# A transformer layer with routed experts: scatters issued one in a round, two PSUM banks for the shared experts' sums, and VectorE making one of the two copies that swap a query's halves

## What is computed

```python
x = x + attention(layernorm(x), freqs_cis, Wq, Wkv_a, kv_gamma, kv_beta, Wkv_b, Wout)
x = x + moe(layernorm(x), gate_w, w_gate, w_up, w_down, sw_gate, sw_up, sw_down)

# inside the attention, for each query
def _rope(x, theta):
    x1, x2 = (x[..., 0::2], x[..., 1::2])
    c, s = (jnp.cos(theta), jnp.sin(theta))
    return jnp.stack([x1 * c - x2 * s, x1 * s + x2 * c], axis=-1).reshape(x.shape)

# inside the mixture: 8 experts, each token goes to its 2 best, and all go through a shared expert
scores = jax.nn.softmax(x @ gate_w, axis=-1)
topk_w, topk_idx = jax.lax.top_k(scores, K)
routed = jnp.einsum('teh,ehd,te->td', silu(gate) * up, w_down, comb)
shared = jax.nn.silu(x @ sw_gate) * (x @ sw_up) @ sw_down
```

## Time and profile before

| | |
|---|---|
| runs | 649.59, 646.07, 648.93 us; median 648.93 |
| the profiled execution | 649.52 us, its span 647.7 us |
| TensorE's mean granted clock | 0.979 of full |
| TensorE busy, matmuls / weight loads | 611.8 us / 594.9 us |
| VectorE, ScalarE, GpSimd busy | 470.3, 475.8, 407.9 us |
| head, until about | 50 us |
| middle loop, until about | 489 us |
| shared expert for batches 0 to 3, until about | 529 us |
| expert tiles, until about | 614 us |

### The profile page before, as it was taken

How to read it: one execution, slowest core, us unless ns; L and a number is a source line. 1 busy time by engine, 2 the same in 40 slices (tenths; PEclk the granted TensorE clock), 3 DMA queues, 4 the chain that set the end, 5 groups by cost and what they waited for, 6 DMA issues and landing times. The chain is left out here.

```text
span 647.7 us, 15727 instructions
## 1 busy us (share of the span) xinstructions
PE 611.8 (94%) x4916; PEld 594.9 (92%) x4916; DVE 470.3 (73%) x1406; ACT 475.8 (73%) x1331; POOL 407.9 (63%) x455
## 2 busy tenths in 40 slices
PE   8989999999899989989999999998987889999995
PEld 7879999999899989989999999998977879999995
DVE  6666786887666877778688887777676676666577
ACT  4669899899688979879888987987864435555531
POOL 2467888786877799689779968967602204444400
PEclk9998999999899999999999999999889999999999
DMA  9891000000100000010000001010302146444283
GB/s 251 250 330 25 2 2 2 2 34 1 35 2 33 26 10 34 2 35 3 34 34 2 34 1 35 1 67 33 123 34 74 70 128 190 130 126 123 84 301 105
DMA packets 34025, 45.41 MB, mean 70 GB/s; under 512 B 4057, under 2 KB 29113, under 8 KB 33945
## 3 DMA queue, kind: packets, MB, share of 16 engines
q1 hardware_dynamic: 29160, 34.56, 17.0%
q0 software_dynamic: 3408, 9.34, 4.4%
q10 hardware_dynamic: 1376, 0.50, 0.3%
HBM read 27.57 MB, written 16.82 MB: 69 GB/s over the span
## 5 line engine op out<-in xcount | busy, mean ns | idle before, releaser
L1239 ACT ACTIVATE probs<-ps_s,nmax 128x256 f32<-128x256 f32 x256 | 119.1, 476 | 10.5 <-DVE nmax L1429 10.2
L1774 POOL TENSOR_TENSOR qswap<-qswap,qsin 128x512 f32<-128x512 f32 x64 | 83.0, 1297 | 50.0 <-ACT qswap L1216 49.8
L224 PE MATMUL ps_q<-xa,wq_hi 128*128 128x256 f32 x512 | 103.0, 299 | 3.1 <-DVE qf L1424 3.1
L1429 DVE TENSOR_REDUCE nmax<-ps_s 128x2 f32<-128x512 f32 x128 | 86.8, 678 | 13.8 <-PE ps_s L224 12.8
L1216 ACT ACTIVATE pT_hi<-ps_t 128x512 fp32r<-128x512 f32 x128 | 76.7, 599 | 22.6 <-PE ps_t L975 21.4
L224 PE MATMUL ps_s<-kT_hi,q_hi 128*128 128x256 f32 x256 | 79.1, 309 | 10.5 <-POOL q_lo L1781 8.4
L1777 POOL TENSOR_TENSOR qf<-qf,qswap 128x512 f32<-128x512 f32 x64 | 82.7, 1292 | 7.9 <-DVE qf L1424 3.5
L1781 POOL TENSOR_TENSOR q_lo<-qf,q_hi 128x512 fp32r<-128x512 f32 x64 | 82.9, 1295 | 7.6 <-ACT q_hi L1216 7.6
L224 PEld LDWEIGHTS ps_q<-xa,wq_hi 128*128 128x128 f32 x512 | 81.6, 196 | 4.8 <-DVE qf L1424 3.3
L297 DVE TENSOR_TENSOR pT_lo<-ps_t,pT_hi 128x512 fp32r<-128x512 f32 x128 | 81.9, 681 | 0.0
L224 PE MATMUL ps_o<-pT_hi,kv_hi 128*128 128x256 f32 x256 | 77.3, 302 | 2.6 <-ACT norm L1216 2.5
(11 more groups left out here) (316 smaller groups left out, 1904.3 us busy)
## 6 DMA issues: line engine op xcount, KB each, us to landing
xg<-routed_in SPq DMA_DIRECT2D x39, 129.0 KB
normal_turned<-xf SPq DMA_DIRECT2D x8, 512.0 KB
wq_raw<-Wq_dram SPq DMA_DIRECT2D x16, 192.0 KB, 4.8
x<-x_dram SPq DMA_DIRECT2D x8, 256.0 KB, 5.8
xa<-normal_turned SPq DMA_DIRECT2D x4, 512.0 KB, 5.7
mgu_hi<-routed_out SPq DMA_DIRECT2D x4, 512.0 KB, 5.2
mgu_lo<-routed_out SPq DMA_DIRECT2D x4, 512.0 KB, 8.0
out_dram<-x SPq DMA_DIRECT2D x8, 256.0 KB, 2.9
```

What stands on the lines that cost most here:

```text
L224: last = nc.tensor.matmul(out, stat, mov, start=start and n == 0, stop=stop and n == len(terms) - 1, skip_group_check=skip)
L1239: last = nc.scalar.activation(probs[h % 3][:, j, :], L.ps_s[h % 2][:, j, :], ACT.Exp, bias=nmax[:, h % NH, j:j + 1], accum_out=rsum[:, h % ...
L1429: vec.tensor_reduce(nmax[:, h % NH, :], L.ps_s[h % 2][:, :, :], AX.X, ALU.max, negate=True).then_inc(ev.max_done, 1)
L1774: gp.tensor_tensor(qs, qs, L.qsin[:, :].unsqueeze(1).to_broadcast([P, 2, S]), ALU.mult).then_inc(ev.qrot_part, 1)
```

## The change

Four things are changed together.

- **Scatters.** `scatter(b, n)` issues one of a batch's four indirect DMAs, behind `rotate` and `query_lo` of its round: at r = 2, 3 and 6 of batch i = b + 2 and at r = 0 of the next; in the last batch at r = 2, 3, 5 and 6. There are two semaphores, for even and odd batches, and the normalized rows lie by turns in xhat_f and xhat_g. The scatters of batches 6 and 7 are issued after the loop, as before.
- **The swap.** ScalarE makes one of the two copies. VectorE makes the other, at the head of `query_cos`, and GpSimd's `rotate` waits for both.
- **Banks.** The shared sums lie by turns in ps_s[0] and ps_t[0], gate and up by turns in ps_q, ps_s[1] and ps_t[1]. The waits of `gate_up`, `down` and `units_turn` follow.
- **Order of TensorE** in the first stretch of the shared expert: each `down` comes one `gate_up` later, and `turn_f`, `logits` and `rank` of the last batch move with it.

```diff
-        xhat_of = [xhat_f] * (B - 1) + [xhat_g]
+        xhat_of = [xhat_f, xhat_g] * (B // 2)
...
-        ps_d = L.ps_s[0]
+        ps_d = L.ps_s[0], L.ps_t[0]
...
         def gu_spot(n):
-            return (L.ps_q, L.ps_s[1])[(n - (n >= ES * FIRST) * ES * FIRST) % 2]
+            return (L.ps_q, L.ps_s[1], L.ps_t[1])[n % 3]
...
                 elif n == 1:
                     pe.wait_ge(ev.exp_done, HEADS)
-                elif n == ES * FIRST:
-                    pe.wait_ge(ev.unit_done, n)
-                else:
-                    pe.wait_ge(ev.unit_done, n - 1)
+                elif n >= 3:
+                    pe.wait_ge(ev.unit_done, n - 2)
...
-                if m == 0 and b >= 1:
-                    pe.wait_ge(ev.acc_done, b)
+                if m == 0 and b >= 2:
+                    pe.wait_ge(ev.acc_done, b - 1)
...
             def units_turn(j):
                 pe.wait_ge(ev.u_done, j + 1)
+                if j == 0:
+                    pe.wait_ge(ev.acc_done, FIRST)
...
+            gate_up(1, 0)
             down(0, 0)
-            gate_up(1, 0)
+            gate_up(1, 1)
             down(0, 1)
+            gate_up(1, 2)
+            down(0, 2)
             turn_f(B - 1)
-            gate_up(1, 1)
-            down(0, 2)
+            gate_up(2, 0)
+            down(1, 0)
             logits(B - 1)
...
                     if n == ES * FIRST + 1:
                         pe.wait_ge(ev.y_done, TILES)
+                    if n == ES * FIRST + 2:
+                        pe.wait_ge(ev.utlo_done, TILES)
...
                 act.wait_ge(ev.q_full, g + 1)
                 if g >= 2:
                     act.wait_ge(ev.qrot_done, g - 1)
-                copy(qswap[g % 2][even, :, :], L.ps_q[odd, :, :])
-                copy(qswap[g % 2][odd, :, :], L.ps_q[even, :, :]).then_inc(ev.qraw_done, 1)
+                copy(qswap[g % 2][even, :, :], L.ps_q[odd, :, :]).then_inc(ev.qraw_done, 1)
...
             def normal_f(b):
                 act.wait_ge(ev.rsf_done, b + 1)
-                if b == B - 1:
+                if b == 1:
                     act.wait_ge(ev.cleared, 16)
-                elif b >= 1:
-                    act.wait_ge(ev.scattered, 64 * b)
-                    act.wait_ge(ev.xf_turned, b)
+                if b >= 2:
+                    act.wait_ge(ev.scattered[b % 2], 64 * (b // 2))
+                    act.wait_ge(ev.xf_turned, b - 1)
...
             def query_cos(g):
+                dve.wait_ge(ev.q_full, g + 1)
+                if g >= 2:
+                    dve.wait_ge(ev.qrot_done, g - 1)
+                vec.tensor_copy(qswap[g % 2][odd, :, :], L.ps_q[even, :, :]).then_inc(ev.qodd_done, 1)
                 dve.wait_ge(ev.qraw_done, g + 1)
...
             def rotate(g):
                 pool.wait_ge(ev.qraw_done, g + 1)
+                pool.wait_ge(ev.qodd_done, g + 1)
...
-            def scatter(b):
-                pool.wait_ge(ev.slots_done, b + 1)
-                pool.wait_ge(ev.tags_done, 2 * (b + 1))
-                pool.wait_ge(ev.xhf_done, b + 1)
-                if b == 0:
+            def scatter(b, n):
+
+                if n == 0:
+                    pool.wait_ge(ev.slots_done, b + 1)
+                    pool.wait_ge(ev.tags_done, 2 * (b + 1))
+                    pool.wait_ge(ev.xhf_done, b + 1)
+                if b == 0 and n == 0:
                     pool.wait_ge(ev.cleared, 16)
-                for k in range(TOP):
-                    for j in range(NT):
-                        gp.indirect_dma_start(xs[:, :], bass.IndirectOffsetOnAxis(L.slots[:, b, k, j:j + 1], 0), xhat_of[b][:, j, :], None
-                                              ).then_inc(ev.scattered, 16)
+                k, j = divmod(n, NT)
+                gp.indirect_dma_start(xs[:, :], bass.IndirectOffsetOnAxis(L.slots[:, b, k, j:j + 1], 0), xhat_of[b][:, j, :], None
+                                      ).then_inc(ev.scattered[b % 2], 16)
...
-                if r == 2 and batch(i - 2):
-                    scatter(i - 2)
                 if pair(g + 3):
                     rotate(g + 3)
                 if pair(g + 2):
                     query_lo(g + 2)
+
+                light = (2, 3, 6, 8) if i < B - 1 else (2, 3, 5, 6)
+                if r in light and batch(i - 2):
+                    scatter(i - 2, light.index(r))
+                if r == 0 and batch(i - 3):
+                    scatter(i - 3, 3)
```

More of the change, by code:

```diff
@@ L68, in __init__ @@
         self.in_loaded = [sem(f"in_loaded{b}") for b in range(B)]
-        self.xf_stored, self.scattered = map(sem, ("xf_stored", "scattered"))
+        self.xf_stored = sem("xf_stored")
+        self.scattered = [sem(f"scattered{n}") for n in range(2)]
         self.out_stored = sem("out_stored")
-        self.q_full, self.qraw_done, self.qcos_done, self.qrot_part, self.qrot_done, self.qhi_done, self.qlo_done = map(
-            sem, ("q_full", "qraw_done", "qcos_done", "qrot_part", "qrot_done", "qhi_done", "qlo_done"))
+        self.q_full, self.qodd_done, self.qraw_done, self.qcos_done, self.qrot_part, self.qrot_done, self.qhi_done, self.qlo_done = map(
+            sem, ("q_full", "qodd_done", "qraw_done", "qcos_done", "qrot_part", "qrot_done", "qhi_done", "qlo_done"))
         self.small_inv, self.rinv_done, self.norm_full, self.norm_done, self.on_done, self.ohi_done, self.olo_done, self.out_done = map(
@@ L922, in _ @@
             sp.wait_ge(ev.table_done, 2)
-            sp.wait_ge(ev.scattered, 64 * B)
+            for n in range(2):
+                sp.wait_ge(ev.scattered[n], 64 * (B // 2))
             for j in range(TILES):
@@ L1065, in down @@
                     pe.wait_ge(ev.exp_done, HEADS)
-                if m == 0 and b >= 1:
-                    pe.wait_ge(ev.acc_done, b)
+                if m == 0 and b >= 2:
+                    pe.wait_ge(ev.acc_done, b - 1)
                 rows = chunk_rows(m)
                 for j in range(NT):
-                    last = three(ps_d[:, j, :], [(u_hi[n % 3][0:rows, tile(j)], u_lo[n % 3][0:rows, tile(j)],
+                    last = three(ps_d[b % 2][:, j, :], [(u_hi[n % 3][0:rows, tile(j)], u_lo[n % 3][0:rows, tile(j)],
                                                        L.sd_hi[0:rows, m, :], L.sd_lo[0:rows, m, :])],
@@ L1167, in _ @@
             rank(B - 2)
+            gate_up(1, 0)
             down(0, 0)
-            gate_up(1, 0)
+            gate_up(1, 1)
             down(0, 1)
+            gate_up(1, 2)
+            down(0, 2)
             turn_f(B - 1)
-            gate_up(1, 1)
-            down(0, 2)
+            gate_up(2, 0)
+            down(1, 0)
             logits(B - 1)
-            gate_up(1, 2)
-            down(1, 0)
-            gate_up(2, 0)
+            gate_up(2, 1)
             down(1, 1)
             rank(B - 1)
-            gate_up(2, 1)
+            gate_up(2, 2)
             down(1, 2)
-            gate_up(2, 2)
+            gate_up(3, 0)
             down(2, 0)
-            gate_up(3, 0)
+            gate_up(3, 1)
             down(2, 1)
-            gate_up(3, 1)
+            gate_up(3, 2)
             down(2, 2)
-            gate_up(3, 2)
             down(3, 0)
@@ L1510, in tokens @@
             def tokens(b):
-                if b == B - 1:
+                if b == 1:
                     dve.wait_ge(ev.cleared, 16)
-                elif b >= 1:
-                    dve.wait_ge(ev.scattered, 64 * b)
+                if b >= 2:
+                    dve.wait_ge(ev.scattered[b % 2], 64 * (b // 2))
                 vec.tensor_scalar(xhat_of[b][:, :, D], L.token[:, :], float(b * TOP * S), None, ALU.add).then_inc(ev.tags_done, 1)
@@ L1585, in accumulate @@
                 done = ev.acc_done if b < B - 1 else ev.fin_done
-                vec.tensor_tensor(L.x2[:, b, :, :], ps_d[:, :, :], L.x2[:, b, :, :], ALU.add).then_inc(done, 1)
+                vec.tensor_tensor(L.x2[:, b, :, :], ps_d[b % 2][:, :, :], L.x2[:, b, :, :], ALU.add).then_inc(done, 1)
             def rows_lo(j):
@@ L1848, in _ @@
             power_f(B - 1)
-            scatter(B - 2)
-            scatter(B - 1)
+            for b in (B - 2, B - 1):
+                for n in range(TOP * NT):
+                    scatter(b, n)
             for j in range(TILES):
```

## The result

The median of six runs is 642.31 us (640.51 to 642.98), that of the kernel before, with three more runs than stood above, 648.31 (646.07 to 649.59): a ratio of 0.9908, 95% interval 0.9886 to 0.9929. That is 6.0 us less, where 13.9 were forecast. The profiled execution took 642.09 us, its span 640.3.

The account below looks back on a forecast made before the run. TensorE, busy 94% of the span, was taken as the bound. The terms -16.95 + 1.0 - 1.5 + 3.0 + 0.3 + 0.5 = -13.65 us put the median near 635.3, stated as 635; range 627 to 645.

Parts of the forecast that it names:

- the old stalls: Middle loop: four scatters and a slot wait on GpSimd delay q_lo, and TensorE with it; excess 16.95 us.
- Rival 1: VectorE's lateness reaches TensorE in a third of the 48 uncovered rounds, 9.6 us in place of 3.0: 642; chance 0.20.
- scatters, with the give-back in batch 7: Loop: spreading scatters returns the whole excess, -16.95 us; batch 7 loses some of TensorE's lead, +1.0.
- ScalarE-limited pairs and VectorE's lateness: Loop: waits for ScalarE's second copy go in five batches, -1.5 us; VectorE's later qf costs +3.0.
- head and batch 0: Head of the kernel: the fourth copy pushes the projection of the fifth pair, +0.3 us.
- first stretch of the shared expert: Before the first expert tile: later turn of the last rows, mostly filling TensorE's waits, +0.5 us, from -3 to +2.
- expert tiles and the second stretch: From 622.78 to 642.54 us: bound by the order and length of VectorE's work, gain 0.
- Rival 4: Loop: a GpSimd wait for VectorE's moments at r = 4 replaces q_lo's; rounds stay 9.5 us: 648; chance 0.05.
- +3.0, half a microsecond in each of batches 2 to 7: Loop: cost of VectorE's copies, one fitting the slack and two in a row less; ends 0 and 10 us.
- My pair of tight rounds: Batch 5, rounds r = 0 and 1: the projection waits for qf; five batches have this pair.
- the 6 that I had named as a sign of being wrong: Whole kernel: the prediction is wrong if TensorE's waits on qf, pT_lo or norm grow past 6 us in all.
- The 52.5 us for a batch without stalls: Loop: a batch should last about 52.5 us once the stalls are gone, against 55.28 in batch 5.

Follow-up runs that it names:

- The cut of q_lo: Changed kernel with GpSimd's q_lo cut to one column in rounds r = 1, 5 and 7 of batches 2 to 7: 637.19 us.
- experiments 1 and 2: Against the kernel before: first, the scatters alone, 631.41 us; second, VectorE's copy alone, 655.73 us.
- the 13 copies of 8: Kernel with the scatters alone, plus VectorE's copy only in rounds r = 0 and r = 5: 627.24 us.
- experiment 6: Kernel with the scatters alone, plus q_lo cut to one column in rounds r = 1, 5 and 7 of batches 2 to 7: 632.77 us.
- the first kernel of 8: Kernel with the scatters alone, plus VectorE's copy in rounds r = 2 to 7: 633.77 us.
- experiments 3 and 4: First, the kernel before with banks and order alone, 657.67 us; second, the changed kernel with the copy back on ScalarE, 634.99 us.
- experiments 5 and 7: Changed kernel: first, q_lo cut to one column in three rounds of batches 2 to 7, 637.19 us; second, both copies on VectorE, 668.42 us.

## Why the prediction was wrong in size

The direction, the cause of the old stalls and the range were right; the forecast of 635.0 was 7.3 too low. Rival 1 named 642, and that its number came is luck in good part: it had the copies' bare 0.60 reach TensorE in 16 rounds, 9.6 - 1.5 = 8.1 us in all. The loop lost 5.72 to the copies, most of it through GpSimd, and the scatters gave 1.3 more than forecast; the stretch before the first tile and the head, 3.2 us above the forecast together, made the number up again. Term by term, the forecast and what the profiles show (batches 1 to 7 by the inverses):

| term | forecast | measured |
|---|---|---|
| scatters, with the give-back in batch 7 | -16.95 + 1.0 | -17.24 alone in the loop |
| ScalarE-limited pairs and VectorE's lateness | -1.5 + 3.0 | +5.72 in the loop |
| head and batch 0 | +0.3 | +1.29 |
| first stretch of the shared expert | +0.5 | +2.66 |
| expert tiles and the second stretch | 0 | +0.2 |

Between the profile's forecast, 635.9, and its 642.09 lie 6.2 us: 2.9 in the loop, 2.2 before the first tile, 1.0 in the head and 0.2 behind. The head's share says little: the six kernels in which ScalarE makes both copies everywhere, the same in that part but for the scatters' buffers, reach the first inverse of batch 1 anywhere from 98.42 to 99.78 us.

- **The scatters.** Right, and the 1.0 of give-back did not come: batch 7 up to its last inverse went from 47.37 to 43.47 us, 3.9 less. The rounds at r = 3 are 7.41, q_lo holds nobody, the half clock at 174 to 180 is gone. Rival 4 fell.
- **The copy. This is the step that failed**: "+3.0, half a microsecond in each of batches 2 to 7". The instruction was under-priced first, 690 ns and 0.72 in the queue where I had 0.60. The 658 ns that I had estimated from the table of the Trainium skill (VectorE: DVE Perf Modes, section on the TRN2 errata) were nearer, and still below the trace's 690. The larger fault was what I took as slack. I priced the copy by its own length against 1.38 us at one projection and left out that it shifts all that stands behind it on VectorE, the operations between SBUF tiles among it, into GpSimd's. The cut of q_lo shows that as 4.6 us. My pair of tight rounds became three in each of batches 2 to 5, r = 0, 1 and 6, and in batch 4 also r = 2, whose projection starts 0.05 or 0.06 us behind qf; at r = 4 0.15 us is left of 1.6. TensorE's waits on qf, pT_lo and norm are 9.2 + 1.2 + 0.6 = 11.0 us, past the 6 that I had named as a sign of being wrong; the sign was badly set, since the kernel before had 3.1 + 1.3 + 2.5 = 6.9. The 52.5 us for a batch without stalls had no working behind it either: with the scatters alone it is 53.8 in batches 2 to 4.
- **The ScalarE-limited pair.** The -1.5 was there to be had, but not in this kernel: VectorE no longer idles for ScalarE, 14.6 us before and nothing of note after, and then is itself late. With the copy only where that cover is, it came, and more: -2.97 in batches 1 to 7 (460.90 - 100.22 = 360.68 against 363.65), -4.2 in the medians.
- **The shared expert.** Forecast +0.5 with a range to +2; measured +2.66. The turn of the last rows starts 22.1 us behind the last inverse and not 20.7, the logits 25.3 and not 24.8, and the slots come 1.15 later. I had said the added work would fill waits that TensorE has anyway. It did, but TensorE then had less left to do during the exponential and the two table loads: 3.1 us of idle time in one piece, and behind it 499 to 505 at half the clock:

```profile
496.00:499.00 3.00, 0.15 (x2) 0.06 (x1) 0.45 (x2) 2.27 (x6) 0.00 (x0) 0.74 0.05 14
499.00:505.00 6.00, 5.79 (x27) 5.80 (x28) 4.09 (x29) 2.06 (x6) 0.00 (x0) 0.50 0.00 0
```

What the stretch costs goes with the clock in it. From the last inverse to the first tile, before and after:

```profile
479.76:530.62 50.86, 42.31 (x308) 39.94 (x309) 33.60 (x134) 20.90 (x51) 11.27 (x13) 0.93 0.19 65
```

```profile
469.48:523.00 53.52, 44.92 (x307) 42.54 (x308) 33.66 (x135) 20.60 (x50) 11.10 (x13) 0.86 0.19 64
```

With the old order four profiles (before, experiments 1 and 2, and the 13 copies of 8) have 50.65 to 50.86 us at a mean granted clock of 0.93, and two more (experiment 6 and the first kernel of 8) 49.3 to 49.4 at 0.97. With the new order three (experiments 3 and 4 and the changed kernel) have 53.47 to 53.52 at 0.86 to 0.87, and two (experiments 5 and 7) 50.4 at 0.92 to 0.93. At about the same clock, 0.92 to 0.93, the new order is thus no longer than the old. What sets it apart is the idle 3.1 us, which all five profiles have, each time with half the clock behind it; no run takes that stall out and leaves the rest of the order. I had no term for the clock there.

- **The second stretch** gained nothing, as forecast; VectorE is as full there as in the earlier trace rows:

```profile
614.70:634.50 19.80, 17.27 (x137) 16.18 (x135) 19.46 (x49) 5.11 (x16) 0.00 (x0) 0.99 0.66 230
```

- **ScalarE** lost 32.4 us of busy time by the page for 64 copies of 37.8. Its instructions overlap on the page, where their durations add up to 90 to 100 us more than its busy time, so "38 less" was too simple.

## What to carry to other kernels

Price a moved instruction by the start-to-start step in its new queue, and then go through what it pushes: which operations behind it meet another engine's, and how much slack is left at each place where the bottleneck waits, not at one. Move work to the fuller engine only in those rounds where it idles for just that work; here 13 copies took 3.0 us off the loop where 64 put 5.7 on it. When a change joins several edits, run each alone: one of the three here was worth 17 us, and the other two together gave back 11. And set the granted clock beside each stretch before a difference of 1 to 5 us is put down to the edit.

## What the runs showed of the hardware that was not expected

- A VectorE operation on SBUF tiles that starts beside one of GpSimd's is held until GpSimd's ends: 1.21 us for 0.17 of work, 1.75 for 0.89, and GpSimd's 0.74 becomes 1.38 in the other direction. Operations out of PSUM kept their length: pT_lo 681 and 682 ns, the maxima 678 and 675, before and after.
- A copy of 32 partitions x 512 from PSUM takes VectorE 690 ns, as long as its product over 128 x 512 (692), and ScalarE 591.
- After the same stall of some 2 us at the scatters TensorE's clock stayed full in some batches and fell to half in others, at 3 us a time. In the stretch before the tiles two executions with the same order differ by 4.8 us, at a mean granted clock of 1.00 and 0.87.
